# Preparation of an attention kernel: values scaled on ScalarE, one key group split and the values widened on GpSimd, turned rows kept in three places, values turned between the first maxima

## The reference

```python
q = (x @ Wq + bq).reshape(1, B * N, H, hd)          # x is layer-normalised; H = 16 heads, hd = 16
kv = (cond @ Wkv + bkv).reshape(1, -1, 2, H, hd)
k, v = (kv[:, :, 0], kv[:, :, 1])
...
q = _fq_sym(q, axis=-1)      # rounded to 255 levels by the largest |.| of each head's 16 numbers
k = _fq_sym(k, axis=-1)
v = _fq_sym(v, axis=2)       # by the largest |.| of a column over all 2048 rows
attn = jnp.einsum('bhqd,bhkd->bhqk', q, k)
attn = jax.nn.softmax(attn.astype(jnp.float32), axis=-1)
attn = _fq_unsigned(attn, axis=-1)
out = jnp.einsum('bhqk,bhkd->bhqd', attn, v)
```

## Time and profile before

| | us |
|---|---|
| median of three runs | 1159.33 (1158.93 to 1160.88) |
| the profiled execution | 1159.07 |
| its span, first to last instruction | 1157.4 |

### The profile page before, as it was taken

How to read it: one execution, slowest core, us unless ns; L and a number is a source line. 1 busy time by engine, 2 the same in 40 slices (tenths; PEclk the granted TensorE clock), 3 DMA queues, 4 the chain that set the end, 5 groups by cost and what they waited for, 6 DMA issues and landing times.

```text
span 1157.4 us, 24150 instructions
## 1 busy us (share of the span) xinstructions
PE 1059.9 (92%) x8396; PEld 603.4 (52%) x8396; DVE 947.1 (82%) x1734; ACT 888.7 (77%) x1544; POOL 699.3 (60%) x625
## 2 busy tenths in 40 slices
PE   7988898889988988998898988999999999999997
PEld 4743444444444444444444446756654465557775
DVE  6999999999999999999999996963327788943335
ACT  4679999999999999999999997645543576834441
POOL 3016888888788887878788778247761000653432
PEclk9999999999999999999999999999999999999999
DMA  6798898887888888988875765847938002523336
GB/s 195 119 168 147 170 171 161 174 174 161 170 176 168 166 163 172 169 158 175 174 116 106 119 110 92 256 136 213 325 111 328 1 1 48 178 87 108 98 97 235
DMA packets 388799, 176.36 MB, mean 152 GB/s; under 512 B 330413, under 2 KB 373650, under 8 KB 388680
## 3 DMA queue, kind: packets, MB, share of 16 engines
q1 hardware_dynamic: 381976, 157.85, 62.6%
q0 software_dynamic: 6480, 16.77, 4.3%
q10 hardware_dynamic: 224, 0.20, 0.1%
HBM read 52.70 MB, written 43.59 MB: 83 GB/s over the span
## 4 chain that ended last, share of the span: by engine, by line
PE 50%; DVE 33%; ACT 5%; issue 5%; DMA 3%; POOL 2%; SPq 1%; POOLq 0%; ACTq 0%; DVEq 0%
DVE top L425 27%; PE bank L234 10%; PE bank L220 9%; PE bank L252 4%; PE bank L2634 4%; PE bank L1598 3%; PE bank L1199 3%; PE bank L2650 3%; PE bank L1186 2%; PE bank L1175 2%; ACT weight L485 2%; PE bank L1871 1%; PE bank L1616 1%; PE bank L682 1%; POOL dispatched_rows L1841 1%
## 5 line engine op out<-in xcount | busy, mean ns | idle before, releaser
L485 ACT ACTIVATE weight<-bank,bias,sq_all 128x1024 uint8<-128x1024 f32 x512 | 609.8, 1201 | 19.1 <-PE bank L234 13.8
L425 DVE TENSOR_REDUCE top<-bank 128x1 f32<-128x512 f32 (+1 forms) x683 | 610.1, 951 | 11.6 <-PE bank L220 1.1
L537 POOL CAST weight<-turned 128x2048 bf16<-128x2048 uint8 x256 | 479.2, 1892 | 36.6 <-DMA turned<-weight 16.1
L234 PE MATMUL bank<-kT,query 128*128 128x512 bf16 x1024 | 307.7, 382 | 12.5 <-ACT weight L485 5.3
L252 PEld LDWEIGHTS bank<-v_sb,weight 128*128 128x128 bf16 x4096 | 172.2, 97 | 103.4 <-POOL weight L537 1.3
L220 PE MATMUL bank<-kT,qspace 64*128 64x512 bf16 x687 | 135.0, 387 | 54.9 <-DVE top L425 54.9
L252 PE MATMUL bank<-v_sb,weight 128*128 128x16 bf16 x4096 | 172.5, 169 | 1.0 <-POOL weight L537 1.0
L220 PE MATMUL bank<-kT,query 128*128 128x512 bf16 x337 | 127.8, 379 | 1.6 <-DVE top L425 1.4
L234 PEld LDWEIGHTS bank<-kT,query 128*128 128x128 bf16 x1024 | 59.7, 96 | 104.4 <-ACT weight L485 62.6
L1841 POOL DMA_INDIRECT dispatched_rows<-qspace,put x32 | 37.1, 1160 | 116.1 <-DVE qspace L2391 106.9
L485 ACT ACTIVATION_READ_ACCUMULATOR weight<-bank,bias,sq_all 128x1 f32 x512 | 101.7, 199 | 0.0
(11 more groups left out here) (351 smaller groups left out, 1458.0 us busy)
## 6 DMA issues: line engine op xcount, KB each, us to landing
dispatched_rows<-zeros SPq DMA_DIRECT2D x32, 524.0 KB, 3.2
answered_rows<-zeros SPq DMA_DIRECT2D x16, 512.0 KB, 3.4
late<-answered_rows SPq DMA_DIRECT2D x16, 512.0 KB, 6.3
erow<-dispatched_rows SPq DMA_DIRECT2D x39, 131.0 KB
wgu<-in_L_ffn_w_gate SPq DMA_DIRECT2D x26, 176.0 KB, 3.3
wgu<-in_L_ffn_w_up SPq DMA_DIRECT2D x26, 176.0 KB, 3.4
query<-qspace SPq DMA_DIRECT2D x32, 128.0 KB, 3.1
turned<-weight SPq DMA_TRANSPOSE x256, 3.1
```

The costliest lines, as they stand in the source:

```text
L234: mm = pe.matmul(unit[u % 2][:, v * 512:(v + 1) * 512], query2[:, t % 2, h, :], kT[:, h // 2, first + v * 512:first + (v + 1) * 512], star ...
L425: ve.tensor_reduce(top[:, first:first + count], bank[:, first % 3:first % 3 + count, :], AX.X, ALU.max).then_inc(s_max, 1)
L485: ac.activation(weight8[:, n % BYTES, u * 1024:(u + 1) * 1024], unit[u], ACT.Exp, bias=bias[:, n:n + 1], scale=sq_all[:, n:n + 1], accum_o ...
L537: po.tensor_copy(weight[:, n % 3, :, :, :].rearrange("p c q two -> p (c q two)"), turned8[:, n % 3, :, :].rearrange("p c q -> p (c q)").bi ...
```

## The change

- vbyte is computed by ACT (scale_values moves from DVE to ACT, as an activation with a scale) and widened by POOL instead of ACT.
- For key group 2, both subtractions (keys without high parts; the low part) move from DVE to POOL. SP and ACT wait for POOL's count for these.
- xnT has three places (late rows 5, 6, 5, 7 for groups 0 to 3) instead of one, so copy_rows waits for what used the place before: for group 2 the projection of group 0, for group 3 POOL's last reading of y2[0]. scale_values waits for the projection of group 1, since its output lies on that group's place.
- The projection of value group 1 goes to banks 6 and 7 instead of 4 and 5, and so turn_rows(3, 4) doesn't wait for its copy.
- Orders: ACT does high(3) ahead of normalise(3), and both scalings behind copy_rows(3). DVE scales key group 3 right behind dividing it, and divides query group 1 ahead of split_last. PE turns the values between the first blocks of scores instead of ahead of them.

```diff
-                xn, xnT = late[:, 4, :].rearrange("p (g c) -> p g c", c=C), late[:, 5, :].rearrange("p (c n) -> p c n", c=CK)
+                xn = late[:, 4, :].rearrange("p (g c) -> p g c", c=C)
+                xnT = [late[:, r, :].rearrange("p (c n) -> p c n", c=CK) for r in (5, 6, 5, 7)]
...
+                pool_count = counted("identity", "padding", ("keys without high parts", 2), ("keys split", 2), ("values rounded", 0), ("values rounded", 1))
... # prepare_sync
-                    sp.wait_ge(s_prep_vector, vector_count["keys split", 2])
+                    sp.wait_ge(sq_["constants_ready"], pool_count["keys split", 2])
                     turn_split(2, keys_split_in[2][0], kT)
... # prepare_tensor
                     turn_rows(1, 0)
-                    project_values(1, 4)
+                    copied(("values", 0))
+                    project_values(1, 6)
                     read(("keys read", 3))
                     turn_rows(2, 2)
                     project_queries(1, 0)
-                    copied(("values", 1))
                     turn_rows(3, 4)
                     project_queries(2, 2)
                     project_queries(3, 4)
-                    copied(("values", 0))
-                    copied(("values rounded", 0))
-                    turn_values(0, 0, 7)
-                    turn_values(0, 1, 6)
-                    copied(("values rounded", 1))
                     read(("queries read", 1))
                     stir(8, 0)
                     read(("queries read", 2))
+                    stir(4, 0)
+                    block = fill_maxima(pe, 0, 3)
+                    copied(("values", 1))
+                    pe.wait_ge(sq_["constants_ready"], pool_count["values rounded", 0])
+                    turn_values(0, 0, 7)
+                    block = fill_maxima(pe, block, 2)
+                    turn_values(0, 1, 6)
+                    block = fill_maxima(pe, block, 1)
+                    read(("queries read", 3))
+                    pe.wait_ge(sq_["constants_ready"], pool_count["values rounded", 1])
                     turn_values(1, 1, 3)
+                    block = fill_maxima(pe, block, 2)
                     copied(("turned values", 0))
                     turn_values(1, 0, 7)
-                    stir(4, 0)
-                    block = fill_maxima(pe, 0, 3)
-                    read(("queries read", 3))
+                    block = fill_maxima(pe, block, 1)
                     while block < LEAD:
... # prepare_vector
                     divide_keys(3)
-                    subtract_high(2)
                     scale_keys(3)
                     measure_values(1)
-                    split_low(2)
                     value_scales()
-                    scale_values(0)
                     subtract_high(3)
-                    scale_values(1)
+                    divide_queries(1, 0)
                     split_last()
-                    divide_queries(1, 0)
                     divide_queries(2, 2)
                     divide_queries(3, 4)
... # prepare_scalar
                     def copy_rows(g, b):
                         ac.wait_ge(s_prep_tensor, tensor_count["rows", g])
-                        if g > 0:
-                            ac.wait_ge(s_prep_tensor, tensor_count["queries", g - 1])
-                        ac.copy(late[:, 5, :], flat(b, b + 2)).then_inc(s_prep_scalar, 1)
+                        if g == 2:
+                            ac.wait_ge(s_prep_tensor, tensor_count["queries", 0])
+                        if g == 3:
+                            ac.wait_ge(sq_["constants_ready"], pool_count["keys split", 2])
+                        ac.copy(xnT[g], flat(b, b + 2).rearrange("p (c n) -> p c n", c=CK)).then_inc(s_prep_scalar, 1)
...
+                    def scale_values(c):
+                        ac.wait_ge(s_prep_vector, vector_count["value scales"])
+                        ac.wait_ge(s_prep_tensor, tensor_count["queries", 1])
+                        ac.activation(vbyte[:, c, :], vT[:, c, :], ACT.Copy, scale=vscale[:, 1, c:c + 1]).then_inc(s_prep_scalar, 1)
...
-                    add_value_bias(1, 4)
+                    add_value_bias(1, 6)
                     middle(2)
+                    high(3)
                     normalise(3)
-                    high(3)
                     copy_rows(2, 2)
                     middle(3)
-                    widen_values(0)
                     copy_rows(3, 4)
-                    widen_values(1)
+                    scale_values(0)
+                    scale_values(1)
                     triple(1)
... # prepare_pool
                     quarter(0)
+                    po.wait_ge(s_prep_scalar, scalar_count["high parts", 2])
+                    po.tensor_tensor(y2[0], y2[0], third(split[1], 0), ALU.subtract).then_inc(sq_["constants_ready"], 1)
+                    po.wait_ge(sq_["constants_ready"], pool_count["keys without high parts", 2])
+                    po.wait_ge(s_prep_scalar, scalar_count["middle parts", 2])
+                    po.tensor_tensor(third(split[1], 2), y2[0], third(split[1], 1), ALU.subtract).then_inc(sq_["constants_ready"], 1)
+                    for c in range(CK):
+                        po.wait_ge(s_prep_scalar, scalar_count["values scaled", c])
+                        po.tensor_copy(vint[:, c, :], vbyte[:, c, :]).then_inc(sq_["constants_ready"], 1)
                     for g in range(1, NG):
                         quarter(g)
```

More of the change, by code:

```diff
@@ L576, in program @@
                                        ("queries", 0), ("high parts", 2), ("normalised", 2), ("rows", 1), ("values", 1), ("middle parts", 2),
-                                       ("normalised", 3), ("high parts", 3), ("rows", 2), ("middle parts", 3), ("values rounded", 0),
-                                       ("rows", 3), ("values rounded", 1), ("queries", 1), ("turned values", 0), ("turned values", 1), ("turned values", 2), ("turned values", 3), "gates",
-                                       ("queries", 2), ("queries", 3))
+                                       ("high parts", 3), ("normalised", 3), ("rows", 2), ("middle parts", 3), ("rows", 3),
+                                       ("values scaled", 0), ("values scaled", 1), ("queries", 1), ("turned values", 0), ("turned values", 1),
+                                       ("turned values", 2), ("turned values", 3), "gates", ("queries", 2), ("queries", 3))
                 vector_count = counted("bias parts", ("statistics", 0), ("inverses", 0), ("keys read", 0), ("keys scaled", 0), ("statistics", 1),
@@ L583, in program @@
                                        ("inverses", 2), ("keys split", 1), ("statistics", 3), ("values measured", 2), ("inverses", 3),
-                                       ("queries read", 0), ("keys read", 2), ("keys scaled", 2), ("keys read", 3),
-                                       ("keys without high parts", 2), ("keys scaled", 3), ("values measured", 1), ("keys split", 2),
-                                       "value scales", ("values scaled", 0), ("keys without high parts", 3), ("values scaled", 1),
+                                       ("queries read", 0), ("keys read", 2), ("keys scaled", 2), ("keys read", 3), ("keys scaled", 3),
+                                       ("values measured", 1), "value scales", ("keys without high parts", 3), ("queries read", 1),
                                        ("keys split", 3, 0), ("keys split", 3, 1), ("keys split", 3, 2), ("keys split", 3, 3),
-                                       ("queries read", 1), ("queries read", 2), ("queries read", 3))
+                                       ("queries read", 2), ("queries read", 3))
+                pool_count = counted("identity", "padding", ("keys without high parts", 2), ("keys split", 2), ("values rounded", 0), ("values rounded", 1))
                 def third(buffer, r):
@@ L694, in project_queries @@
                         pe.wait_ge(s_prep_scalar, scalar_count["rows", g])
-                        project(0, xnT, wq, b)
+                        project(0, xnT[g], wq, b)
                     def project_values(g, b):
@@ L948, in middle @@
                     def middle(g):
-                        ac.wait_ge(s_prep_vector, vector_count["keys without high parts", g])
+                        if g == 2:
+                            ac.wait_ge(sq_["constants_ready"], pool_count["keys without high parts", 2])
+                        else:
+                            ac.wait_ge(s_prep_vector, vector_count["keys without high parts", g])
                         ac.copy(third(split[keys_split_in[g][0]], 1), y2[g % 2]).then_inc(s_prep_scalar, 1)
```

7 lines of the change are left out of this document (1 added, 6 removed).

## The result

The changed kernel takes 1164.54 us (1162.80 to 1168.23) against 1159.38 us (1158.93 to 1160.88) of the kernel before, seven runs each on one chip: a ratio of 1.0048, with a 95% interval of 1.0034 to 1.0063. It is slower by 0.5%, where 1159.1 and a range to 1161.5 were forecast. The profiled execution took 1164.54 us, with a span of 1162.8. The fastest of the seven has a span of 1161.1 and a mean granted clock of 0.995; the three slowest, at 1166.5 to 1168.2 us, have 0.991 or 0.992.

A forecast was written before the change was run, and what follows sets the result against it. DVE's maxima, in step with ACT's exponentials, were taken as the bound. A 2.8 us earlier first maximum, all but 0.15 taken back at head 4, plus slight catching up gave span 1157.4 - 0.25, median 1159.1 us; range 1156.5 to 1161.5.

The forecast's parts named there:

- What bounds the kernel: Attention: DVE maxima and ACT exponentials in step for 630 us; a DVE gain must pass ACT's first heads.
- S = 67.95: End of preparation: DVE's first maximum starts at 67.95 us instead of 70.76, 2.8 us earlier.
- So this costs nothing until a subtraction takes more than 3.9 us: Preparation: POOL's two subtractions, taken at 2.9 us each, delay the first maximum only by what exceeds 3.9 us.
- low bound: Preparation: least time for one 128x1024 subtraction on POOL, 2.3 us, without a fixed part in each.
- the preparation's sum: Preparation: 1.9 us from DVE's order and 0.9 from PE's bring the first maximum 2.8 us earlier.
- The wait at head 4: ACT's head 4: late values delay head 0's bytes to 27.4 us after the first maximum; ACT stands about 2.7 us.
- shift = S - 68.1: Whole kernel: if the wait at head 4 binds, the time shifts by the first maximum's start minus 68.1.
- 0.2 to 0.5 us that DVE was to be ahead: Behind head 4: DVE can be 0.2 to 0.5 us ahead as ACT catches up.
- Rival C: PE's stop of up to 2.5 us at head 4 lowers the granted clock, costing 2 to 3 us: 1161.8; chance 0.04.
- Rival A: Head 4: the wait is smaller and the 2.8 us gain is kept, 1156.5 us; chance 0.17.
- D: Preparation: group 3's projection isn't moved, first maximum 69 or so, late values cost 1 us: 1160.2; chance 0.05.
- B: Preparation: GpSimd is slow at its two subtractions; 1160.9 us at 5.6 us each, 1162.3 at 7; chance 0.20.

The follow-up runs named there:

- both parts moved back: Changed kernel with key group 2's two subtractions back on VectorE and the widenings back on ScalarE; 1161.30 us, ratio 1.0016 to the kernel before.
- stirs: Changed kernel with 12 extra identity matmuls on PE ahead of the unit where it stops for head 4; 1164.03 us, ratio 1.0035.
- widening on ScalarE: Changed kernel with the widenings back on ScalarE, key group 2's subtractions staying on GpSimd; 1163.15 us, ratio 1.0019.
- subtractions on VectorE: Changed kernel with key group 2's two subtractions back on VectorE, the widening staying on GpSimd; 1161.07 us, ratio 1.0001.
- one idle subtraction: Kernel before with one more GpSimd instruction, a 128x1024 float32 subtraction of zeros whose result nobody needs; 1162.06 us, ratio 1.0005.
- values first: Changed kernel with PE turning all values ahead of the first maxima, as before; moves to GpSimd and ScalarE stay; 1158.66 us, ratio 0.9992.
- both with the first copy ahead: Changed kernel, nothing moved to GpSimd; ScalarE does first values copy, query group 2's tripling, other copies, group 3's tripling, then tanh; 1157.92 us, ratio 0.9979.
- queries ahead: Changed kernel with ScalarE tripling query group 2 ahead of the values copies, group 3 right behind them, tanh last; 1161.50 us, ratio 1.0006.

## Why the prediction was wrong, point by point

- What bounds the kernel: right. The shift of the fifth join was that of the 65th to 0.05 us in every kernel but one (both parts moved back: +0.02 and +0.62), and DVE's gain had to pass ACT's first heads.
- S = 67.95: wrong, 70.17. The step that failed is "So this costs nothing until a subtraction takes more than 3.9 us". Both subtractions were short (2.14 and 2.26 us, below the low bound of 2.3), and they cost VectorE 2.5 us all the same, because only GpSimd's own delay was priced. The row that the step rested on the earlier trace rows was read as GpSimd held up by VectorE; in the rows here the one that began second waited, and the case with GpSimd first wasn't asked for. Nor were the widenings set beside split_last: 2.1 us. Of S, the subtractions alone took 0.9 us (68.76 for 67.83), the widenings alone nothing (67.83), and both together 2.3.
- The rest of the preparation's sum was right: with the contention gone S is 67.83, and PE's projection is what it waits for. VectorE had the room for the two subtractions: with them back, it still waits 0.15 us for PE at 60.7 and 0.59 at 64.6. So their move could gain nothing at S; the sum, which had VectorE waiting at both places, gave reason to ask.
- The wait at head 4: right in kind and nearly in size. Forecast was S + 27.4; measured, in the five kernels where it binds, S + 27.9 (changed), 27.8 (stirs), 27.7 (widening on ScalarE) and 26.8 (twice, where the subtractions are on VectorE). The rule shift = S - 68.1 gives +2.1 for the measured S; head 4 stands at +2.55. With the values ahead of the maxima the wait is gone, as it was worked out.
- Of the 0.2 to 0.5 us that DVE was to be ahead behind the wait, nothing is to be seen: with both parts moved back it goes from -0.84 at head 4 to +0.02 at the fifth join. The head behind waited there as well and the clock was low for some 3 us, and the run doesn't tell the two apart. The sum also wrote -0.25 where its own rule, S - 68.1, gives -0.15.
- Rival C, the granted clock, was given 0.04 and came true at once with the stop: some 0.8 us of the lasting shift, by the run with stirs, where C had 2 to 3. This is the second step that failed: the forecast put the clock's part at nothing. It wasn't a rival to the forecast but a follow-up of it: the forecast itself had PE stop for 2.5 us. The chance of the range's upper end had to be taken from there. The low clock at 743 us is another thing (below).
- Rival A (the gain is kept) didn't occur, nor D, as the S of 67.83 without contention shows that the projection of group 3 had moved; B had the right direction by another mechanism: GpSimd wasn't slow, it was in the way. In size no one of these is the whole: by the forecast's own rule the measured S of 70.17 gives 1161.4 us; the longer wait and what comes behind it make it 1163.1 (1159.33 + 3.75), and the fall at 743 us the rest.

The sum after the fact, against the spans: -2.8 as forecast for S, +2.2 for the contention, +3.15 for the wait at head 4 (from -0.6 to +2.55), +1.2 behind it (0.8 of it the clock's), +1.3 to 1.8 at 743 us: 5.1 to 5.6, measured 5.4. Against the forecast span of 1157.15 the miss is 5.65 us: 2.2 for the contention, 0.45 for the wait at head 4 being longer than the rule has it, 1.2 behind it, some 1.65 at 743 us, and 0.1 for the slip from -0.15 to -0.25.

**What stays open.** Why the clock fell at 743 us in the profiled execution, where PE's work and gaps are as before but for 3.75 us of time; the kernel before shows lower mean clocks too in some of its runs. Falls within 735 to 746 or 785 to 793 us stand in six of the eight experiments' traces as well, among them three in which PE has no stop at head 4 (one idle subtraction, values first, and both with the first copy ahead). With the values first it lasted from 737 to 743.7 us:

```profile
737.00:743.50 6.50, 6.50 (x20) 4.43 (x21) 6.26 (x32) 4.43 (x10) 2.94 (x4) 0.50 1.15 310
```

So such a fall comes without the stop at head 4, and with the first copy ahead it came without the moved work on GpSimd. The other six timed executions of the changed kernel have no trace, so whether it has such falls more often than the kernel before stays open.

## What to carry to other kernels

An instruction moved to an idle engine has to be set beside what the busy engine runs at that time, in both directions: here 8.5 us of work on GpSimd took 4.6 us from VectorE, through three instructions of 0.2 us and one of 0.4. A step that is turned later is to be followed through every queue behind it (PE, ACT, SP, DMA, ACT again) until something waits for it; its slack is a number that can be read off, and a gain ahead of it that doesn't move it is lost. And if a forecast has TensorE stop for 2 us, the lower clock belongs into the forecast and not among its rivals.

## What the runs showed of the hardware that I had not expected

- A VectorE multiply of 128x64 float32 in SBUF is held until the end of a GpSimd subtraction that starts 7 to 10 ns ahead of it (1.94 to 2.18 us for 0.20), as is one of 128x2 (0.66 for 0.17); a subtraction with two SBUF inputs is held by a GpSimd widening that began before it (2.11 for 0.42) and not by one that began behind it (0.42). Reductions of one input, from SBUF (1.22 us beside the second subtraction) or PSUM (1.21 beside a widening), aren't.
- All four stops of PE at head 4, of 1.8 to 2.8 us, went ahead of a fall of the granted clock to half, and where stirs filled the stop it stayed full. It was at half at once behind 2.83 us (changed kernel, for 5 us) and behind 1.78 us (both parts moved back), within 2 us behind 1.77 us (subtractions on VectorE), and behind 2.65 us (widening on ScalarE) the first pair was still at full clock and the window 100 to 104 us was at 0.50. Behind a stop of 2.26 us, earlier in the kernel, its mean was 0.59 with the queries ahead and stayed at 1.00 in the changed kernel.
- A subtraction of 128x1024 on GpSimd took 2.14 us with one strided bf16 input, 2.26 with a strided bf16 output as well, and 1.90 with one tile of float32 as both inputs and output.
